# Attention scores on four row groups of the PE array, expert choice in the bank of transposed probabilities, and a new order of the attention loop

## What is computed

```
xn = layernorm(x)
Q = xn @ Wq.T + bq;  K = ctx @ Wk.T + bk;  V = ctx @ Wv.T + bv      # 16 heads of 16
energy = einsum('bhqd,bhkd->bhqk', Q, K) / 4, masked keys -> -1e10
x = x + tanh(g_xattn) * ((softmax(energy) @ V) @ Wfc.T + bfc)
xn2 = layernorm(x)
w = softmax of the top 2 of xn2 @ gate_kernel, 0 for the other experts
x = x + tanh(g_ffn) * sum_e w[e] * ((silu(xn2 @ w0[e]) * (xn2 @ w1[e])) @ wo[e])
```

## Time and profile before

| | us |
|---|---|
| median of 3 runs (1422.74 to 1425.14) | 1425.06 |
| the profiled execution | 1419.93 |
| its span in the trace | 1418.3 |
| attention phase with its start and its end, in the trace | about 0 to 740 |
| expert phase, in the trace | about 740 to 1418 |

### The profile page before, as it was taken

The page is one execution under the profiler, slowest core; times in us unless marked ns, Lnnn a source line. Parts: engine busy times, 40 slices in busy tenths (PEclk is TensorE's granted clock), DMA queues, the critical chain, the costliest instruction groups (busy, mean ns, idle before and its releaser), DMA issues.

```text
span 1418.3 us, 35550 instructions
## 1 busy us (share of the span) xinstructions
PE 1332.4 (94%) x9634; PEld 1168.6 (82%) x9635; DVE 808.1 (57%) x2522; ACT 695.4 (49%) x1778; POOL 890.7 (63%) x1389
## 2 busy tenths in 40 slices
PE   6999999999999999999829999999999999999996
PEld 5888888888888888888718888888888888888885
DVE  5688788888887887887733333333333333333332
ACT  3666666656666666666613333333333333333332
POOL 5588888888888888888853444444444444444443
PEclk9999999999999999999959999999999999999998
DMA  4133332233332333322677884333333333333332
GB/s 151 41 102 121 122 119 75 96 122 119 113 109 71 110 123 126 111 90 83 219 211 207 216 220 77 53 53 54 52 56 52 54 54 55 52 54 50 55 56 34
DMA packets 73956, 139.70 MB, mean 98 GB/s; under 512 B 11585, under 2 KB 55137, under 8 KB 71745
## 3 DMA queue, kind: packets, MB, share of 16 engines
q0 software_dynamic: 32064, 52.46, 19.0%
q1 hardware_dynamic: 39840, 86.05, 18.6%
q10 hardware_dynamic: 2016, 0.74, 0.2%
HBM read 68.95 MB, written 70.27 MB: 98 GB/s over the span
## 4 chain that ended last, share of the span: by engine, by line
PE 56%; issue 12%; DVE 11%; POOL 11%; ACT 4%; DMA 3%; DVEq 1%; POOLq 1%; SPq 0%; another core or an unknown queue 0%; ACTq 0%
PE banks L1322 25%; PE psB L1341 13%; PE banks L1156 4%; PE psT L1330 4%; POOL routed_rows L484 3%; PE psG L1307 2%; ACT prob L608 2%; PE banks L1108 2%; PE psT L1168 2%; ACT prob L612 2%; DMA out_dram<-ey,eid 2%; DVE qT L827 2%; POOL rs L426 1%; POOL rs L462 1%; POOL wrec L475 1%
## 5 line engine op out<-in xcount | busy, mean ns | idle before, releaser
L1322 PE MATMUL banks<-w_all,etT 128*128 x1620 | 433.2, 403 | 0.7 <-ACT etT L725 0.7
L1058 DVE TENSOR_TENSOR hgT<-psT,hgT 128x512 fp32r<-128x512 f32 x135 | 93.4, 692 | 425.0 <-ACT hgT L737 377.8
L1322 PEld LDWEIGHTS banks<-w_all,etT 128*128 128x128 f32 x1620 | 286.3, 189 | 51.3 <-issue 3.6
L537 POOL DMA_INDIRECT out_dram<-ey,eid x135 | 216.5, 1604 | 121.2 <-issue 46.1
L532 POOL DMA_DIRECT2D et<-routed_rows x135 | 79.2, 586 | 265.4 <-issue 202.3
L1341 PEld LDWEIGHTS psB<-w_all,hgT 128*128 128x128 f32 x1620 | 208.4, 188 | 18.4 <-issue 1.3
L1341 PE MATMUL psB<-w_all,hgT 128*128 x1620 | 217.9, 283 | 0.8 <-ACT hgT L737 0.8
L743 ACT ACTIVATE ey<-psB,ewt 128x256 f32<-128x256 f32 x135 | 64.0, 474 | 234.3 <-PE psB L1341 168.4
L731 ACT ACTIVATE hs<-banks 128x512 f32<-128x512 f32 x135 | 80.7, 597 | 185.5 <-PE psT L1330 183.6
L437 POOL TENSOR_TENSOR kbd<-kT,own 128x616 fp32r<-128x616 f32 x128 | 152.2, 1219 | 20.7 <-DVE kT L849 20.7
L1180 PE MATMUL psB<-vbd,probT 128*128 128x51 f32 x1280 | 158.1, 271 | 0.0
(11 more groups left out here) (163 smaller groups left out, 2307.1 us busy)
## 6 DMA issues: line engine op xcount, KB each, us to landing
split_weights<-w_part SPq DMA_DIRECT2D x16, 1536.0 KB
w_all<-split_weights SPq DMA_DIRECT2D x32, 768.0 KB
et<-routed_rows POOLq DMA_DIRECT2D x135, 129.0 KB
xb<-in_x_dram SPq DMA_DIRECT2D x32, 256.0 KB, 2.8
w_raw<-in_L_ffn_w_kernel_dram SPq DMA_DIRECT2D x32, 256.0 KB
out_dram<-x SPq DMA_DIRECT2D x64, 128.0 KB
w_raw<-in_L_ffn_wo_kernel_dram SPq DMA_DIRECT2D x16, 256.0 KB
cb<-in_ctx_dram SPq DMA_DIRECT2D x32, 77.0 KB
```

The lines of the kernel that those rows point to most:

```text
L537: gp.indirect_dma_start(out=out, out_offset=bass.IndirectOffsetOnAxis(ap=eid[:, u:u + 1], axis=0), in_=ey[:, u % 2, :], in_offset=None, co ...
L1058: dve.tensor_tensor(hgT[:, 1].rearrange("p c q -> p (c q)"), psT[:], hgT[:, 0].rearrange("p c q -> p (c q)").bitcast(F32), ALU.subtract).t ...
L1322: m = pe.matmul(banks4[:, bank], etT[:, u % 2, a, c], weight(e, c, w, n), start=(j == 0), stop=(j == len(steps) - 1))
```

## The change

The width of 128 partitions is now seen as four row groups of 32. A row group of one half `c` of the width holds two heads, so a spread block is 2 x 77 = 154 columns. Each of four banks holds the four heads of one row group, two for each half `c`. `scores` issues 4 mask matmuls of 308 columns and 24 matmuls of 154 columns, all with 32 contracted rows, in the order row group 0, 1, 2, 3, to four different banks. To bring the right heads to the right rows, the columns of the transposed `Wk` and `Wq` are permuted when they are copied, and `bq` and `bk` go through DRAM in permuted order before they are loaded. Keys move to the bank of the attention output (`psB`), the projected output to that of `n2_T` (`psG`), and logits and ranks to the upper half of `psT`, from where one ACT copy (`gated_evac`) takes both to SBUF. `weigh` runs once for two tiles. The orders of PE, ACT, DVE and POOL are rewritten: DVE takes the four-head maximum first and puts the small steps of the choice between the large ones, POOL takes four scatters together in every second tile.

```diff
@@ constants @@
+    ROWS = 32
+    HP = ROWS // HD
+    RG = P // ROWS
+    HB = HP * DC
+    S_BANKS = [(n, h, HB) for n, h in enumerate(range(0, H, HB))]
+    S_FULL = RG - 1
+    PAIR = HP * K2
-        kbd = sb("kbd", [P, 2, 2, DC, HC, K2], F32R)
+        kbd = sb("kbd", [P, 2, 2, DC, HP, K2], F32R)
+        psK = psB[:, H * VW:H * VW + DC * K2]
+        psLR, psL, psR = psT[:, D:D + 3 * E], psT[:, D:D + E], psT[:, D + E:D + 3 * E]
+        psY = psG[:, D:2 * D]
@@ POOL: spread_keys @@
-                for a, c in ((a, c) for a in range(2) for c in range(DC)):
-                    gp.tensor_tensor(kbd[:, u, a, c], kT2[:, a, c].bitcast(F32).rearrange("p (o k) -> p o k", o=1).to_broadcast([P, HC, K2]),
-                                     own[:].rearrange("p (h o) -> p h o", o=1).to_broadcast([P, HC, K2]), ALU.mult).then_inc(kbd_done, 1)
+                for a in range(2):
+                    gp.tensor_tensor(kbd[:, u, a], kT2[:, a].bitcast(F32).rearrange("p c (o k) -> p c o k", o=1).to_broadcast([P, DC, HP, K2]),
+                                     own2[:].rearrange("p (o s l) -> p o s l", o=1, l=1).to_broadcast([P, DC, HP, K2]), ALU.mult).then_inc(kbd_done, 1)
@@ POOL: batch @@
                     if known(i, 2):
+                        rstd_2(i - 2)
+                    if t == 0:
+                        for q, r in (((n - 1, 1), (n - 1, 2)) if u == 0 else ((n, 0),)):
+                            if known(q, 0):
+                                split_low(q, r)
+                        if known(b, 2):
+                            number_rows(i - 4, u4)
+                            number_rows(i - 3, u4 + 1)
+                        if more:
+                            spread_keys(b + 1, 1 - u)
+                        if more2:
+                            rstd_1(b + 2)
+                    else:
+                        if known(b, 2):
+                            weigh(b - 2, u)
+                            scatter(i - 5, u4 - 1, b - 2)
+                            scatter(i - 4, u4, b - 2)
+                        if more:
+                            residual(b + 1, 1 - u, n + u)
@@ ACT: start @@
+            for n, v in enumerate((bq, bk)):
+                act.dma_start(by_quarter[n].rearrange("c (j q) -> c j q", j=RG), v.rearrange("(j c q) -> c j q", c=DC, q=ROWS)).then_inc(staged, 16)
...
+                act.wait_ge(staged, 32)
+                for n in (1, 0):
+                    for a in range(DC):
+                        act.dma_start(bias[:, n, a:a + 1], by_quarter[n, a].rearrange("(q o) -> q o", o=1)).then_inc(const_in, 16)
@@ ACT: gated_evac instead of l_evac; in batch behind exp_scores @@
+                if known(i, 1):
+                    act.wait_ge(r_ps, i)
                     act.wait_ge(l_idx, i)
+                act.copy(gated[:, first:last], psLR[:, first:last]).then_inc(l_cp, 1)
@@ DVE: batch @@
+                    if softmax:
+                        s_largest(i + 1, 1 - t, 1)
+                    if known(i, 2):
+                        stats_2(i - 2, t, 1)
                     if keys:
                         k_evac(b + 1)
...
                     if softmax:
+                        s_negate(i + 1, 1 - t)
+                    if chosen_now:
+                        choose(i - 3, 1 - t, 0)
+                    if softmax:
                         s_largest(i + 1, 1 - t, 0)
+                    if chosen_now:
+                        choose(i - 3, 1 - t, 1)
                     if keys:
                         k_split(b + 1, 0)
...
+                        place(i - 4, u4, 0)
                     if softmax:
                         s_shift(i + 1, 1 - t)
+                    if chosen_now:
+                        choose(i - 3, 1 - t, 4)
+                    if placed:
+                        place(i - 4, u4, 1)
                     if t == 0 and more:
                         q_low(b + 1, 1 - u)
+                    if chosen_now:
+                        choose(i - 3, 1 - t, 5)
@@ PE: scores @@
-                for n, h, k in S_BANKS:
-                    pe.matmul(psS[:, n, 0:k * K2], share[:], mrow[:, u].rearrange("p (o k) -> p o k", o=1).to_broadcast([P, k, K2]),
+                for j in range(RG):
+                    r0 = j * ROWS
+                    pe.matmul(psS[:, j, 0:HB * K2], share[r0:r0 + ROWS], mrow[r0:r0 + ROWS, u].rearrange("p (o k) -> p o k", o=1).to_broadcast([ROWS, HB, K2]),
                               start=True, stop=False, skip_group_check=True)
...
+                for q_part, k_part in PARTS:
+                    for c in range(DC):
+                        for j in range(RG):
+                            r0 = j * ROWS
+                            m = pe.matmul(psS[:, j, c * PAIR:(c + 1) * PAIR], qT[r0:r0 + ROWS, u, q_part, c, t * P:(t + 1) * P],
+                                          kbd[r0:r0 + ROWS, u, k_part, c].rearrange("p h k -> p (h k)"),
+                                          start=False, stop=True, skip_group_check=True)
@@ PE: prob_T, n2_T, batch @@
+                if g == 0 and known(i, 3):
+                    pe.wait_ge(l_cp, i - 2)
...
+                if below(i, NT - 1):
+                    pe.wait_ge(oT_sb, DC * (i + 2))
...
                     attend(i, u, b, 1)
-                    attend(i, u, b, 2)
                     if known(i, 2):
                         n2_T(i - 2, (u4 - 2) % 4)
+                    attend(i, u, b, 2)
...
                     if known(i, 2):
                         gate(i - 2)
+                    if known(i, 3):
+                        rank(i - 3)
+                    if t == 0 and more:
+                        values(b + 1)
                     if t == 1 and more2:
                         x_T(b + 2)
...
                     if more2:
-                        if known(i, 1):
-                            pe.wait_ge(x1_done, i)
+                        pe.wait_ge(o_sb, i + 1)
```

More of the change, by code:

```diff
@@ L516, in _ @@
             batches(gp, batch)
[L517 to L519 removed]
+            rstd_2(NT - 2)
             rstd_2(NT - 1)
[L521 to L526 removed]
+            for i in range(NT - 4, NT):
+                number_rows(i, i % 4)
+            weigh(B - 2, 0)
+            scatter(NT - 4, 0, B - 2)
@@ L528, in load_rows @@
+            scatter(NT - 3, 1, B - 2)
+            weigh(B - 1, 1)
+            scatter(NT - 2, 2, B - 1)
+            scatter(NT - 1, 3, B - 1)
+            for r in range(1, FR):
+                split_low(NQ - 1, r)
             def load_rows(t, u):
@@ L949, in _ @@
             q_low(0, 0)
-            stats_1(1, 1, 0)
+            for part in range(2):
+                stats_1(1, 1, 0, part)
             for part in range(3):
@@ L953, in _ @@
             late_constants()
-            for part in range(2):
-                s_largest(0, 0, part)
+            s_largest(0, 0, 1)
             s_negate(0, 0)
+            s_largest(0, 0, 0)
             s_shift(0, 0)
@@ L1025, in _ @@
+            stats_2(NT - 2, 0, 1)
+            residual_1(NT - 1, 1, 1, B - 1)
+            for part in range(2):
+                stats_2(NT - 1, 1, part)
+            for i in range(NT - 3, NT):
+                route(i)
+            for part in range(2):
+                free_rows(NT - 1, part)
+            for part in range(3):
+                place(NT - 1, 3, part)
+            dve.wait_ge(base_done, NT)
             steps = [0]
```

388 lines of the change are left out of this document (197 added, 191 removed).

## The result

The changed kernel takes 1366.5 us (median of 4 runs, 1361.8 to 1370.0) where the kernel before takes 1425.1 us: ratio 0.959, 95% interval 0.958 to 0.961. Forecast were 1350 us, between 1310 and 1410. The profiled execution took 1363.92 us, its span is 1362.3 us.

What follows compares the result with a forecast made beforehand. PE's own work, 20.6 us a batch, was taken to set the attention loop's period. 74 us less in the loop, + 1.5 at the start, - 3 at the end gave 1344.4 us, as a median 1350; range 1310 to 1410.

Steps and rivals of the forecast that it cites:

- The block of scores: PE's mask matmuls and score products of a tile: 1.1 us instead of 2.38, sparing 2.56 us a batch.
- The lower end: Lower bound for the block of scores: loads and matmuls of the four row groups overlap fully, 0.8 us.
- the rival with partial overlap: Loads of the row groups overlap in part: block 1.75 us, period about 20.1 us, 1378 us in all; chance 0.18.
- The slower rival: Weight loads stand in line at 107 ns each: block 3.1 to 3.5 us, 1437 to 1465 us in all; chance 0.17.
- The period: Time of one attention batch: 19.2 us instead of 21.6, from halves of 10.2 and 8.5 us plus 0.5 us for DVE.
- DVE as next bound: In the attention loop DVE keeps its 17.7 us of work a batch and is next to bound; 0.5 us added.
- The new order hides nearly all: Rival: period 17.9 us, DVE faster since POOL disturbs it less, 115 us less, 1310 us; chance 0.07.
- the one I had at 0.2 to 0.4 us: Added wait in the short half: late rstd_2, and norm_2 keeps ACT from copying the third group of probabilities.
- Loop in all: Attention loop over 31 batches, each 21.6 - 19.2 us shorter: 74 us less.
- The start: Before the first scores: two transfers to DRAM and a wait ahead of six bias loads, 1.5 us later, 0 to 4.
- The end: After the last batches: rstd_2 first and all eight scatters behind it, about 3 us earlier, 0 to 5.
- Splitting of weights moves within POOL and ACT behind work that is not waited for: Step on the splitting of weights on POOL and ACT: its move was given no cost in the sum.

Runs made afterwards that it cites:

- Experiment 1: Changed kernel with the score products issued one row group after the other instead of in turn; 1447.5 us, ratio to before 1.019.
- Experiment 8: Changed kernel with five more operations of 308 elements a batch on POOL into a buffer that nothing reads; 1457.7 us.
- Experiment 3: Changed kernel with the six bias loads on SP behind its four attention weight loads, instead of on ACT; 1400.4 us, ratio 0.987.
- Experiment 2: Changed kernel with POOL's last weight splittings moved from behind the last scatters to between the last two tiles' rstd_2; 1395.9 us, ratio 0.983.
- experiment 7: Changed kernel without early fetches of expert weights, all of them issued behind the pads; 1424.7 us.
- the early tail and the early start together: Changed kernel with the last splittings between the last two rstd_2 and the bias loads on SP; 1395.2 us on the third chip.
- experiment 10: Changed kernel with the second tile's two scatters moved to the end of POOL's next turn, so they go out two by two; 1505.2 us.
- experiment 9: Changed kernel with DVE's choice and placing each in one piece behind the tile's scores' work, not woven between; 1458.2 us, fourth chip.
- experiment 5: The changed kernel itself, unaltered, run once more on the third chip; 1407.7 us, ratio to before 0.993.

## Why the prediction was right or wrong

**The block of scores: right, size 0.2 us too long.** 0.88 us against 1.1 (bounds 0.8 to 3.1). The lower end is almost met: of the 0.3 us for filling and emptying the array at most 0.1 us shows. Experiment 1 shows the mechanism and gives the price of its absence, 1.74 us, by chance that of the rival with partial overlap. The slower rival's 3.1 us needs 107 ns for each pair of load and matmul; even one row group after the other a pair took 1.70 / 24, 71 ns, and in turn 35 ns. So the 107 ns did not carry over to the scores. They were read from pairs with 128 rows and plain fp32 operands (`probT` and `vbd`), while the scores' operands are fp32r with 32 rows; which of the two differences counts, no run shows. Of the two rules that stood against each other, the trace bears out that of the Trainium skill, TensorEngine Tiling (Array Packing), section Key Properties: tiles load and multiply in parallel. The other, that a load of 32 rows takes as long as one of 128 (the Trainium skill, TensorE: Matmul & The Clock Gate, section LDWEIGHTS), is left open: 71 ns is less than the 107 ns of full rows, but the types differ too.

**The period: right, 18.6 instead of 19.2 us, for another reason in part.** PE's work is 0.957 x 18.6 = 17.8 us (forecast 18.0). The halves are 10.5 and 8.0 (10.2 and 8.5). The step that failed is DVE as next bound, with 0.5 us in the sum: I kept its 17.7 us a batch, and it has 323.4 us in 400, at 21.5 batches 15.0 us, some 80% busy where I wanted 91%. Its operations became shorter: the kT splits had 561 and 696 ns on average before and have 233 and 310 now. That is what the rival "The new order hides nearly all" said of DVE. PE's remaining waits are 0.47 us for ACT's copy and 0.19 us for norm_2. The first is the one I had at 0.2 to 0.4 us, but it stands in the long half, not in the short one; none stands ahead of `rank` or of the first transposes, where I had looked for them. It is PE that bounds the loop still.

**POOL: right.** Two operations of 702 ns (forecast 810), POOL at 73 of 100 us, 13.6 us a batch (forecast 14.0). Experiment 8 shows what more work there costs, most of it by the clock.

**Loop in all: -76.7 against -74 us.** That they agree so well is luck. The steady batch is 0.6 us better than forecast, some 18 us in 31. Against this stand four stretches at the lower clock that I had not foreseen, about 12 us, and the first batches: before, four of them had only 18.3 to 21.3 us, so that the 31 took 662.8 us and not 31 x 21.6 = 669.6, and there was less to gain.

**The start: mis-sized, +4.2 instead of +1.5 us.** I priced six issues at 0.45 us. The four from the permuted copy had 5.42 us together, 1.36 each, on ACT's queue, and the first normalisation moved from 7.70 to 13.01 us. Their form, one word a partition, is not the reason: that of the earlier trace rows is the same, with 0.45 us each. My own upper bound, 4 us, was just too low. Experiment 3 shows the cause. On SP the same four took 2.40 us. Why they took longer on ACT stays open.

**The end: wrong sign, +16.7 instead of -3 us.** The step that failed is "Splitting of weights moves within POOL and ACT behind work that is not waited for". In the last batch it is waited for, by three steps one after another: store, pads, load of routed rows. Experiment 2 returns 10.1 of the 10.2 us. I had followed POOL's order there only up to the scatters, not past SP's queue. The other 6.5 us, up to the last ranks: the wait of 4.42 us for `rstd_2`, which stands behind four scatters when PE has no work of a next batch left, and the lower clock behind it, with PE's steps at twice their time. The scatters in a row I had seen and put at nothing ("I price this below" has no price). That the fetches are not its cause is shown (experiment 7); what share the wait has and what the clock, isn't, since no run took the wait away.

**Where the forecast holds.** On the first chip. On the third the same kernel is 41 us slower and gains 0.7% on before instead of 4.1%; its variants on the second and fourth have the same waits. With its 1407.7 us it is still within 1310 to 1410 us, but the loop's -74 us is not: there the loop is 629.4 us. No row of before could show this: its trace is of the first chip, where the changed kernel has no such waits either. The kernel before has the scatters in two pairs and is not slower on the other chips; that the pairs are the reason isn't shown.

## What to carry to other kernels

Issue matmuls of different row groups, each with a PSUM bank of its own, in turn: with 32 rows each, four groups did in 0.88 us what took 1.74 us one group after the other and 2.38 us with full rows, at the same count of columns. When a step is moved "behind work that nobody waits for", follow it through the last iteration, queue by queue up to the next phase; and when an edit delays the release of a buffer, count how long PE will stand, since the lower clock behind that can cost more than the wait. Measure an edit beside the kernel that it alters, on the same chip: between chips the changed kernel differed by 41 us, while the early tail and the early start together gave 12.5.

## What was new about the hardware

*One kernel, two times.* The kernel before took 1418 to 1425 us in all five groups of runs; the changed one 1366.5 us in one and 1407.7 us in another. What differs are waits with no releaser in this core's trace: 1.2 us of PE a batch, and a maximum of DVE that begins 2.9 us behind its scores, where four indirect transfers in a row enclose the burst of scores. Splitting the row took those of PE in the key projection away and halved those of DVE and ACT on a chip that has them (experiment 10). Whether the chip or the occasion makes the difference, and by what, stays open.

*A small operation of DVE can take as long as POOL's beside it.* The timelines of the changed kernel and of experiment 9:

```profile
321.14 1.27 POOL L500 TENSOR_TENSOR w_part<-w_raw,w_part 128x512 fp32r<-128x512 f32 x1
321.21 1.22 DVE L976 TENSOR_TENSOR chosen<-expert_f,topf 128x16 f32<-128x16 f32 x1
```

```profile
457.11 1.27 POOL L500 TENSOR_TENSOR w_part<-w_raw,w_part 128x512 fp32r<-128x512 f32 x1
457.15 1.25 DVE L987 TENSOR_TENSOR pos<-gated,base 128x8 f32<-128x8 f32 x1
```

Sixteen and eight elements, 0.16 and 0.15 us elsewhere, end with POOL's operation. A cast of kT, which has one input, did the same in experiment 5:

```profile
461.57 1.28 POOL L500 TENSOR_TENSOR w_part<-w_raw,w_part 128x512 fp32r<-128x512 f32 x1
461.69 1.26 DVE L884 CAST kT<-kT 128x154 fp32r<-128x154 f32 x1
```

It has 1211 ns on average there and 233 on the first chip, with the same code: what counts is whether the two meet. The Trainium skill, GPSIMD Engine Reference, section Specifications, says that POOL shares its SBUF interfaces with VectorE, with contention for VectorE's instructions that have two SBUF inputs or run in a 2-port mode. The first two pairs of rows agree with that; in which mode the cast ran, no trace here shows.

*The clock can fall in a loop with short idle times only.* In the changed kernel PE waited 0.47 us up to 148.97 us, as it does in every batch, and had the lower level from there to about 156 us; the projection behind it took 2.04 us instead of 1.09. The other three stretches of the loop begin at the same wait (282, 323 and 473 us). Most batches with this wait keep the higher level, and so does the loop of the kernel before, with waits of 0.5 us in its batches: 1.00 from 200 to 600 us. No run here tells which waits are followed by a fall.
